# One core, a transformer block of two attentions and an MLP: layer norms spread over several periods of the pipeline, their small steps and low parts on other engines

## What is computed

```python
attn_in = adaln(x, cond, ln1, g1, b1)
x = attn(attn_in, attn_in, sa) + x
cross_in = adaln(x, cond, ln1, g1, b1)
ctx_n = ln(context)
x = attn(cross_in, ctx_n, ca) + x
ffn_in = adaln(x, cond, ln2, g2, b2)
x = gelu(ffn_in @ w1 + b1) @ w2 + b2 + x
```

## Time and profile before

| | us |
|---|---|
| median of 3 runs | 1227.95 (1226.4 to 1228.6) |
| the profiled execution | 1228.63 |
| its span in the profile | 1226.8 |
| PE matmuls busy | 1121.1 (91%) |
| DVE busy | 906.9 (74%) |
| POOL busy | 701.5 (57%) |
| ACT busy | 630.3 (51%) |
| mean granted clock of TensorE | 0.973 of full |

### The profile page before, as it was taken

How to read it: one execution, slowest core, us unless ns; L and a number is a source line. 1 busy time by engine, 2 the same in 40 slices (tenths; PEclk the granted TensorE clock), 3 DMA queues, 4 the chain that set the end, 5 groups by cost and what they waited for, 6 DMA issues and landing times.

```text
span 1226.8 us, 18768 instructions
## 1 busy us (share of the span) xinstructions
PE 1121.1 (91%) x6888; PEld 793.8 (65%) x6888; DVE 906.9 (74%) x1128; ACT 630.3 (51%) x861; POOL 701.5 (57%) x538
## 2 busy tenths in 40 slices
PE   3469899888999999999999999999999999985998
PEld 3346666665666666666665666666666666653997
DVE  2467787687787788788888887788778878865443
ACT  3235555555555555556556555555555555665221
POOL 1367575666666666676777666666666666763000
PEclk9689999999999999999999999999999999997999
DMA  5111211221112111211112111211121111110001
GB/s 167 34 35 36 64 31 42 49 54 46 36 35 69 36 36 36 61 40 27 27 36 65 35 35 35 66 36 35 36 65 35 36 35 47 41 35 1 18 18 35
DMA packets 65690, 52.37 MB, mean 43 GB/s; under 512 B 29120, under 2 KB 48576, under 8 KB 65344
## 3 DMA queue, kind: packets, MB, share of 16 engines
q1 hardware_dynamic: 63712, 49.59, 16.3%
q10 hardware_dynamic: 1888, 1.59, 0.4%
HBM read 15.22 MB, written 2.10 MB: 14 GB/s over the span
## 4 chain that ended last, share of the span: by engine, by line
PE 76%; DVE 9%; issue 5%; ACT 5%; POOL 2%; DMA 2%; SPq 1%; ACTq 0%; POOLq 0%; DVEq 0%
PE ps L725 16%; PE ps L590 11%; PE ps L592 10%; PE ps L591 10%; PE ps L703 5%; PE ps L713 5%; PE ps L678 4%; PE ps L790 4%; PE ps L684 4%; PE ps L680 4%; PE ps L682 4%; DVE neg_max L888 3%; DVE w_lo L875 1%; ACT z L418 1%; PE ps L600 1%
## 5 line engine op out<-in xcount | busy, mean ns | idle before, releaser
L460 ACT ACTIVATE probs<-ps 128x1024 f32<-128x1024 f32 x256 | 262.4, 1026 | 216.4 <-PE ps L684 196.8
L888 DVE TENSOR_REDUCE neg_max<-ps 128x2 f32<-128x1024 f32 x256 | 299.2, 1220 | 48.3 <-PE ps L703 48.3
L361 POOL TENSOR_TENSOR acc<-acc,probs 128x1024 f32<-128x1024 f32 x128 | 304.8, 2381 | 16.6
L369 POOL TENSOR_TENSOR eo<-tmp 128x512 f32<-128x512 f32 x64 | 92.6, 1447 | 250.2 <-DVE tmp L914 248.9
L725 PE MATMUL ps<-probs,v 128*64 128x512 f32 x1024 | 230.7, 592 | 0.0
L356 POOL TENSOR_TENSOR acc<-probs 128x1024 f32<-128x1024 f32 x64 | 152.7, 2386 | 90.5 <-ACT probs L460 90.5
L725 PEld LDWEIGHTS ps<-probs,v 128*64 128x64 f32 x1024 | 73.6, 137 | 145.7 <-issue 145.7
L914 DVE TENSOR_TENSOR tmp<-ps,rope 128x1024 f32<-128x1024 f32 x128 | 151.1, 1215 | 15.3 <-PE ps L592 15.3
L703 PE MATMUL ps<-hi 64*128 64x512 f32 x512 | 114.7, 438 | 18.2 <-ACT v L492 9.0
L590 PE MATMUL ps<-xn_hi,w_hi 128*128 128x512 f32 x256 | 109.7, 428 | 21.6 <-issue 10.2
L678 PE MATMUL ps<-max_rows,pick 64*128 64x512 f32 x512 | 111.4, 424 | 4.6 <-DVE o_lo L901 3.5
(11 more groups left out here) (107 smaller groups left out, 2224.4 us busy)
## 6 DMA issues: line engine op xcount, KB each, us to landing
lo<-eo SPq DMA_DIRECT2D x512, 64.0 KB, 2.0
w_raw<-pack_dram SPq DMA_DIRECT2D x16, 192.0 KB, 3.4
x<-x_dram SPq DMA_DIRECT2D x4, 512.0 KB, 11.0
w_raw<-pack_dram SPq DMA_DIRECT2D x8, 256.0 KB, 4.2
max_rows<-neg_max SPq DMA_DIRECT2D x128, 2.0 KB, 2.0
w_raw<-w_dram SPq DMA_DIRECT2D x2, 1024.0 KB, 5.6
out<-x SPq DMA_DIRECT2D x4, 512.0 KB, 2.9
ctx_in<-ctx_dram SPq DMA_DIRECT2D x4, 384.0 KB, 3.7
```

What stands on the lines that cost most here:

```text
L361: pool.tensor_tensor(acc[:, g % 2, :, :], acc[:, g % 2, :, :], probs[:, i, :, :], ALU.add).then_inc(added, 1)
L460: act.activation(probs[:, i, :, :], score_ps(i), ACT.Exp, scale=SCALE).then_inc(exped, 1)
L888: dve.tensor_reduce(neg_max[:, g % 2, :, i], peak_ps(i), AX.X, ALU.max, negate=True).then_inc(maxed, 1)
```

## The change

Each norm gets four numbers, `norm_at[n]`: the period of its statistics, of its rows, of its turning, and whether all three are in one period. Norms 1 to 3 and 8 to 11 have one period for all (-3, -1, 1 and 27, 29, 31, 33). The context's have three in a row (5, 6, 7, then 9, 10, 11, 13, 14, 15 and 17, 18, 19), and norms 12 to 14 too (59, 60, 61, then 61, 62, 63 and 63, 64, 65). The low part follows in the period after the turning, on Pool, in front of its sums. ACT makes the guess as exp(-0.5 ln(var + eps)), and one Newton round remains (6 small instructions instead of 14). In the one-period norms ACT makes guess and rows in front of `high_o` and `keep_av`, and Pool its small steps between the second and third sum; otherwise the guess follows `keep_av`, and Pool's steps follow the third sum. PE always projects first, then turns, then makes the output projection or V. The two banks of a turning change places. The next context is loaded after the rows, in the rows' period. All loops over periods go two further, to 66.

```diff
@@ banks, semaphore
-            return ps[:, (7, 6 if n == LAST else 1)[r], :]
+            return ps[:, (6 if n == LAST else 1, 7)[r], :]
@@ plan
-        stats_in = {-3: 1, -1: 2, 1: 3, 5: 4, 7: 5, 9: 6, 11: 7}
...
+        norm_at = {n: (2 * n - 5, 2 * n - 5, 2 * n - 5, True) for n in range(1, NB)}
         for b in range(NB):
-            stats_in[QUADS - 5 + 2 * b] = norm_of(X, 1, b)
-            stats_in[2 * QUADS - 5 + 2 * b] = norm_of(X, 2, b)
-        del stats_in[2 * QUADS + 1]
-        turned_in = {p + 1: n for p, n in stats_in.items()}
-
-        STATS = 2 * TT + 2
-        STEPS = 4 * NEWTON + 2
+            norm_at[norm_of(C, 0, b)] = (5 + 4 * b, 6 + 4 * b, 7 + 4 * b, False)
+            p = QUADS - 5 + 2 * b
+            norm_at[norm_of(X, 1, b)] = (p, p, p, True)
+        norm_at[norm_of(X, 2, 0)] = (PAIRS - 5, PAIRS - 4, PAIRS - 3, False)
+        norm_at[norm_of(X, 2, 1)] = (PAIRS - 3, PAIRS - 2, PAIRS - 1, False)
+        norm_at[norm_of(X, 2, 2)] = (PAIRS - 1, PAIRS, PAIRS + 1, False)
+        stats_in = {at[0]: n for n, at in norm_at.items()}
+        rows_in_period = {at[1]: n for n, at in norm_at.items()}
+        turned_in = {at[2]: n for n, at in norm_at.items()}
+        low_in = {at[2] + 1: n for n, at in norm_at.items()}
+
+        STATS = 2 * TT + 1
+        STEPS = 6
@@ shared helpers
-        def invert_root(eng, n):
...
+        def refine_rstd(eng, n):
+            eng.wait_ge(ln_guess, 2 * n + 2)
+            eng.tensor_tensor(newton[:, :], rstd[:, :], rstd[:, :], ALU.mult).then_inc(ln_newton, 1)
...
+            eng.tensor_scalar(centre[:, :], newton[:, :], -1.0, None, ALU.mult).then_inc(ln_newton, 1)
+
+        def norm_split(eng, n, r):
...
+            eng.wait_ge(ln_scaled, 2 * n + r + 1)
+            eng.tensor_tensor(low[0:rows, b, r, :], y[0:rows, r, :], high[0:rows, b, r, :], ALU.subtract)\
+               .then_inc(ln_split, 1)
@@ sync
-                n = turned_in.get(p)
+                n = rows_in_period.get(p)
                 if n is not None and order[n][0] == C and order[n][1] + 1 < NB:
                     sp.wait_ge(ln_rows, TT * (n + 1))
                     load_ctx(order[n][1] + 1)
@@ gpsimd, period(p)
+                if p in low_in:
+                    norm_split(pool, low_in[p], 0)
+                    norm_split(pool, low_in[p], 1)
                 if is_pair(p):
                     add_probs(p, 1)
                     add_probs(p, 2)
                 n = stats_in.get(p)
-                if n is not None:
-                    invert_root(pool, n)
+                if n is not None and norm_at[n][3]:
+                    refine_rstd(pool, n)
                 if is_pair(p):
                     add_probs(p, 3)
+                if n is not None and not norm_at[n][3]:
+                    refine_rstd(pool, n)
                 if is_job(p + 4):
                     rotate(p + 4)
+                n = rows_in_period.get(p)
                 if n is not None and order[n][0] == X:
                     add_bias(n)
@@ scalar
+            def guess_rstd(n):
+                act.wait_ge(ln_step, STATS * (n + 1))
+                act.activation(rstd[:, :], var_eps[:, :], ACT.Ln).then_inc(ln_guess, 1)
+                act.wait_ge(ln_guess, 2 * n + 1)
+                act.activation(rstd[:, :], rstd[:, :], ACT.Exp, scale=-0.5).then_inc(ln_guess, 1)
@@ scalar, period(p)
                 if is_pair(p + 2):
                     high_qk(p + 2)
+                n = stats_in.get(p)
+                at_once = n is not None and norm_at[n][3]
+                if at_once:
+                    guess_rstd(n)
+                    norm_rows(n)
                 if is_pair(p - 1):
                     high_o(p - 1)
                 if is_pair(p):
                     keep_av(p)
-                n = turned_in.get(p)
-                if n is not None:
-                    norm(n, 0)
-                    norm(n, 1)
-                if p in stats_in:
-                    norm_rows(stats_in[p])
-                if p % 2 == 1 and is_quad(u + 1):
-                    keep_v(u + 1, 0)
-                    keep_v(u + 1, 1)
+                if n is not None and not at_once:
+                    guess_rstd(n)
+                keeps_v = p % 2 == 1 and is_quad(u + 1)
+                for r in range(2):
+                    if p in turned_in:
+                        norm(turned_in[p], r)
+                    if keeps_v:
+                        keep_v(u + 1, r)
+                n = rows_in_period.get(p)
+                if n is not None and not norm_at[n][3]:
+                    norm_rows(n)
                 if p in split_in:
                     split_weights(*split_in[p])
@@ scalar, start and end
             split_weights(0, 1)
+            guess_rstd(0)
             norm_rows(0)
...
+            guess_rstd(LAST)
             norm_rows(LAST)
@@ tensor
                 if r == 0:
                     pe.wait_ge(ln_rows, TT * (n + 1))
+                    p = norm_at[n][2] if n in norm_at else -1
+                    if p > 0:
+                        pe.wait_ge(av_kept, min(p + 1, PAIRS))
...
                     if g - 1 in turned_in:
-                        pe.wait_ge(ln_scaled, 2 * turned_in[g - 1] + 2)
+                        pe.wait_ge(ln_scaled, 2 * turned_in[g - 1] + 1)
...
                     if i == 1 and p - 1 in turned_in:
-                        pe.wait_ge(ln_scaled, 2 * turned_in[p - 1] + 1)
+                        pe.wait_ge(ln_scaled, 2 * turned_in[p - 1] + 2)
@@ tensor, period(p)
                 if is_pair(p + 1):
                     pe.wait_ge(maxed, 4 * (p + 1) + 4)
+                if is_job(p + 4):
+                    project(p + 4)
                 n = turned_in.get(p)
                 if n is not None:
-                    if is_pair(p):
-                        pe.wait_ge(av_kept, p + 1)
                     norm(n, 0)
                     norm(n, 1)
-                out_first = n is not None and order[n][0] == X
-                if not out_first and is_job(p + 4):
-                    project(p + 4)
                 if p % 2 == 0 and is_quad(u - 1):
                     project_out(u - 1, 0)
                     project_out(u - 1, 1)
-                if out_first and is_job(p + 4):
-                    project(p + 4)
                 if p % 2 == 1 and is_quad(u + 1):
@@ vector, norm_stats
-                dve.wait_ge(ln_step, STATS * n + 2 * TT + 1)
-                dve.tensor_scalar(rstd[:, :].bitcast(I32), var_eps[:, :].bitcast(I32), -0.5, RSQRT_GUESS,
-                                  ALU.mult, ALU.add).then_inc(ln_step, 1)
@@ vector, period(p)
                 if is_pair(p - 1):
                     normalise(p - 1)
                     low_o(p - 1)
-                if not stats_now and is_pair(p + 2):
+                if n is None and is_pair(p + 2):
                     low_qk(p + 2)
-                n = turned_in.get(p)
-                out_first = False
-                if n is not None:
-                    norm_split(n, 0)
-                    norm_split(n, 1)
-                    out_first = order[n][0] == X
-                if not out_first and is_job(p + 4):
+                if is_job(p + 4):
                     rotate(p + 4, 0)
                     rotate(p + 4, 1)
-                if stats_now and is_pair(p + 2):
+                if n is not None and is_pair(p + 2):
                     low_qk(p + 2)
@@ vector, start (the end alike, with LAST)
             norm_stats(0)
-            invert_root(dve, 0)
+            refine_rstd(dve, 0)
```

More of the change, by code:

```diff
@@ L395, in _ @@
             add_bias(0)
-            for p in range(FIRST, PAIRS + 1):
+            for p in range(FIRST, PAIRS + 3):
                 period(p)
@@ L857, in norm_stats @@
                 dve.tensor_scalar(var_eps[:, :], mean_var[:, :, 1], EPS, None, ALU.add).then_inc(ln_step, 1)
-                dve.wait_ge(ln_step, STATS * n + 2 * TT + 1)
-                dve.tensor_scalar(rstd[:, :].bitcast(I32), var_eps[:, :].bitcast(I32), -0.5, RSQRT_GUESS,
-                                  ALU.mult, ALU.add).then_inc(ln_step, 1)
-            def norm_split(n, r):
-                kind, b, _ = order[n]
-                rows = source(n)[1]
-                high, low = (xn_hi, xn_lo) if kind == X else (ctx_hi, ctx_lo)
-                dve.wait_ge(ln_scaled, 2 * n + r + 1)
-                dve.tensor_tensor(low[0:rows, b, r, :], y[0:rows, r, :], high[0:rows, b, r, :], ALU.subtract)\
-                   .then_inc(ln_split, 1)
             def split_weights(w, m):
@@ L938, in period @@
                         peak(p + 1, i)
-                stats_now = p in stats_in
-                if stats_now:
-                    norm_stats(stats_in[p])
+                n = stats_in.get(p)
+                if n is not None:
+                    norm_stats(n)
                 if is_pair(p - 1):
@@ L960, in period @@
                     add_out(u - 1, 1)
-                if out_first and is_job(p + 4):
-                    rotate(p + 4, 0)
```

(3 more changed lines are left out.)

41 lines of the change are left out of this document (17 added, 24 removed).

## The result

The changed kernel takes **1189.47 us** (median of 4 runs, 1187.36 to 1192.91); the kernel before took 1227.97 (4 runs, 1226.4 to 1228.6). The ratio is 0.9691, with a 95% interval of [0.9666, 0.9716]. That is 38.5 us less, where 32 were forecast. The profiled execution took 1189.7 us, its span is 1187.9.

A forecast was written before the change was run, and what follows sets the result against it. Without norms only PE's work counts; gains lie in PE's holes where norms are turned. Context 18.0, x norms 0, start 9.3 and end 4.9 sum to 32.2 off 1228.6: 1196.4, 1196 as a median; range 1184 to 1210 us.

The forecast's parts named there:

- Steps: Small root steps on Pool: 6 instead of 14, 2.2 us less; the guess on ACT 0.5 with its wait.
- rival D: Guess on ACT: Ln and Exp load a table each, 41 us in all, giving 1237 us; chance 0.01.
- Low parts on Pool: Two 128x512 instructions of 1.29 us, 2.6 at the head of Pool's period, so low_qk meets Pool's third sum.
- the 0.65 us: Cost counted for each x norm because low_qk stands beside Pool's third sum; 0.2 for each context norm.
- Rival C: Pool's low parts take 2.28 us each, not 1.29, delaying sums, low_qk, rotate and maxima: 1232 us; chance 0.03.
- Context norms: Periods 6 to 13: excess 25.4 us, minus 7.4 cost once statistics no longer wait for the context; gain 18.0.
- where a weight split follows it is 0.7 more: On ACT and DVE behind the turnings of periods 11 and 19: 0.7 us more for each of the two.
- x norms: Periods 27 to 33: PE waits 1.75 us, then 2.3 in three, for keep_av; cost 17.9 against 17.7, gain 0.
- Rival A: One-period norms: PE's waits trip the clock, 5 x 2.4 = 12 us more, giving 1208; chance 0.22.
- Rival B: x norms: waits stay as short as before and low_qk meets no sum, 8.65 and 2.6 less: 1185; chance 0.17.
- Start: Up to period 3's end: norm 0 1.8 us later, project(2) 2.9 earlier, period 0 12.4 long; gain 9.3.
- End: Period 60 to the first GELU: turnings, V stall and slow stretch go, period 63 starts 4.6 earlier; gain 4.9 us.

The follow-up runs named there:

- w_hi first: Changed kernel with ACT's high half of a weight split right behind keep_av instead of behind the norm and V copies: 1180.95 us, ratio 0.9623.
- the rows behind keep_av: Changed kernel with ACT making guess, o_hi, keep_av and only then the rows in one-period norms: 1187.92 us, ratio 0.9684.
- the dates alone: Kernel before with only the context norms' statistics moved to periods 5, 9, 13, 17, turned as before one period after their rows: 1212.1 us, ratio 0.9888.
- the old root: Changed kernel with DVE's seed and 14 Pool steps back and no guess on ACT: 1214.04 us, ratio 0.9903.
- both ends: Changed kernel with norm 0 rooted on DVE by seed and three rounds, and the second feed-forward split one period later: 1185.88 us, ratio 0.9666.
- the old order in norms 1 to 3: Changed kernel with norms 1 to 3 turned one period after their rows, as before: 1203.57 us, ratio 0.9803.
- the old order in the x norms: Changed kernel with norms 8 to 11 turned a period after their rows, output projection before project, low parts on DVE: 1199.94 us, ratio 0.9781.

## Why the prediction was right, and where its terms were off

The forecast of 1196 had the right mechanism in the context norms and at the start, and the range held; 6.5 us of gain were left out. That is a net of errors which partly cancel: 3.8 too little was counted at the start, 4.2 in the x norms and 0.7 behind the first GELU, 1.1 too much in the context norms and 1.1 at the end. By its own steps:

- **Steps: the prices were right, their worth was not seen.** Six at 0.27 (forecast 0.28); the guess 0.44 with its wait (0.5). Two table loads, so rival D falls. But the step was costed alone. In the old schedule it is worth 6 us, in the new one 24.6: it keeps the waits of the one-period x norms at 1.5 us instead of 3.4, and at 3.4 the clock fell each time.
- **Low parts on Pool: priced right (1.28 against 1.29), their effect on PE not.** The meeting that was forecast for low_qk came: in periods 28, 30, 32 and 34 low_qk stands beside one of Pool's sums and takes 2.10, 2.14, 2.11 and 1.92, not the 1.22 of a free one. What did not come are the 0.65 us that this was to cost PE. Periods 31, 33 and 35 reach their averages after 5.82, 5.77 and 5.74, like a plain one, where before, with low_qk at 3.34, 3.36 and 3.14, it took them 6.40, 6.39 and 6.38. DVE's timeline in period 30, and Pool's:

```profile
560.33 2.14 DVE L923 TENSOR_TENSOR lo<-lo,hi 128x1024 fp32r<-128x1024 f32 x1
...
558.98 5.76 POOL L371 TENSOR_TENSOR acc<-acc,probs 128x1024 f32<-128x1024 f32 x2
```

  How long low_qk is held depends on how far the sum has got when it begins, and PE feels it only beyond some 2.1 us. In the runs above, 2.19, 2.53, 2.78 and 3.06 were followed by averages after 5.88, 6.18, 6.44 and 6.73 (with w_hi first, but for the 2.78, which is of the rows behind keep_av). So the mechanism behind the 0.65 is right, and in the changed kernel it stops just short of costing anything. Rival C (2.28 for a low part) falls.

- **Context norms: 18.0 forecast, 16.9 measured.** The wait for the DMA, the V stall and the slow windows went as said, and the run with the dates alone gives 15.8 of it. The norm itself is cheaper than the 1.5 us put down (periods 7, 11, 15, 19 take 16.43, 16.01, 16.50, 16.01 against 15.25, on average 1.0). The weight splits are dearer: 0.7 was forecast for each of two, those that follow the turnings of 11 and 19; periods 10, 12, 18 and 20 took 0.84, 1.70, 0.94 and 1.72 over 15.25, 5.2 in all. The step "where a weight split follows it is 0.7 more" saw ACT's 3.1 us of evacuations in front of w_hi, but not that DVE, which has nothing else there, waits 3.46 for it with its maxima behind; and it has no term for 10 and 18, where the low half meets Pool's rotation. In the run with w_hi first all four periods are at 15.0.
- **x norms: 0 forecast, 4.2 measured.** The wait is 1.46 in 27 where 1.75 was forecast, and 1.46 to 1.47 in 29, 31 and 33 where 2.3 was, 2.8 less in all; the 0.65 is not paid, 2.6 more. The four periods took 17.67, 18.81, 17.72 and 17.70, where 18 to 19 were named. On the other side period 28 took 17.92, 2.7 over a plain one, where the sum had about 1.6, since the two instructions of the weight split took 3.12 beside Pool's bias. Over the kernel one such instruction takes 0.41 us at the least and 2.60 at the most, as the summary of that tile shows (ns, least/median/most, first and last start):

```profile
L893 DVE TENSOR_TENSOR w_lo<-w_raw,w_hi x32: 411/646/2595, 19.3 to 908.3; 128x256 fp32r<-128x256 f32 x32
```

  The Trainium skill, "SBUF — State Buffer", section "Who interferes with whom", says that a DVE instruction with two SBUF inputs contends with a GpSimd one that reads SBUF and that the later one waits for the whole of the earlier. The trace agrees: the difference of 2.2 us is more than the instruction itself and near the length of one of Pool's with two inputs (2.56 for the bias), and in period 10 above it is the one that begins second, DVE's or Pool's, that is longer.
- **Rival A did not come in the x norms, but was near.** Their four waits of 1.46 left the clock at 1.00 in all of 27 to 35; the old root's 3.38 brought it down. In two other kernels, with w_hi first and with both ends, it fell at period 31 with waits of 1.46 and 1.52, and in the one with the old order in norms 1 to 3 at period 33 with 1.48; each cost 1.6 us. Rival B held in part: the waits were near today's 1.28, and low_qk cost PE nothing, though it did meet a sum. But its 1185 takes off all 8.65 us of the waits and not what they exceed today's by, so the sum of that rival was wrong: the waits are 5.9 us, 2.8 less than forecast. By that, with the 2.6, it would have come to 1191.
- **Start: 9.3 forecast, 13.1 measured.** The guess did delay norm 0 (rows at 19.41, 1.56 later, forecast 1.8), and project(2) started at 53.66 (forecast 54.2). Period 0 starts at 75.09, not 77.1; norm 2's turning, just ahead of V, waits 0.72 for its rows, and which term of those 2.0 was too large is not shown. It reaches its averages in 4.88, not 6.05, and took 11.46 where 12.4 was forecast; periods 1 to 3 took 48.62 where 49.5 was. That periods 0 to 3 hang on the one-period norms is shown by the run with the old order: all of the gain in them goes.
- **End: 4.9 forecast, 3.8 measured.** Period 63 starts only 2.2 earlier against period 60's start, where 4.6 was forecast, and then gives 1.6 where 0.3 was. Period 61 took 17.12. PE's timeline shows what the sum did not have there: the last job was projected in period 59, so the turning follows the averages at once and waits 2.39 for keep_av, and right behind it, from 1040.1, come 3.4 us at the lower clock; without the slow stretch 61 took 15.64 and 15.62, in the kernels with rows behind keep_av and with both ends, though the same wait stands there (2.38 and 2.42):

```profile
1038.87 1.06 PE L634 MATMUL ps<-ident,z 128*128 128x128 f32 x8 [2.39 <-ACT av L502]
```

  The wait ahead of the last projection is the 8.98 shown above.

The runs' differences don't add up: the dates alone give 14.3 in their rounds, while taking the cheap root, the low parts or the place of the turning out of the changed kernel costs 24.6, 9.6 and 4.9. Their sum, 53, is more than the 38.5 that there are. So what a part is worth depends on which others are there.

**Left open.** Why the clock falls behind one wait and not behind another of the same length was not settled. Whether the weight splits could go to periods without a norm was not tried.

## What to carry to other kernels

Spread a norm over periods by first asking which wait each of its instructions brings to the queue that it stands in: moving one load's consumer away from the load brought 15.8 of the 38.2 us up to the first GELU, and one place in ACT's queue was worth 21 us. When a short chain is put on an engine in front of the copies that free buffers, cost what stands behind it on the same engine for another engine's use (here w_hi), not only the copies themselves. A saving that is covered in one schedule can be the one that carries the next, so test parts in both.

## What the runs showed that was not expected

- The length of a wait alone does not decide whether PE's clock falls. At period 31, 1.47 left it at 1.00 in one kernel and 1.46 brought 3.4 us at 0.50 in another; at period 61, 2.39 brought it down, and 2.42 and 2.60 did not. In the kernel with the old order in the x norms, 2.27 ahead of period 30's turning brought 3.4 us at 0.50 and 2.28 ahead of 32's none. At 3.4 it fell all five times, for 3.4 to 6.8 us, so that 1.9 us more of wait cost 3.5 to 4.8 us a norm. What decides between equal waits is not shown.
- Ln and Exp of 128x4 take 0.21 us each, as little as DVE's and Pool's steps of that shape (0.17 and 0.20), and need no further table load.
- Two low parts of 128x512 take 3.49 us on DVE beside Pool's rotation and bias, and 2.68 on Pool, where they stand behind these and beside DVE's maxima. Alone one takes 0.69 on DVE and 1.28 on Pool, so the engine that is faster when alone was the slower one here.
- Which of the two engines begins first, by less than 0.1 us, decided whether a weight split took 0.69 or 1.78 us on DVE, and whether the next period took 15.00 or 16.09.
